# Alternating the convolution's matmul groups with the transposes on TensorE, more of the scaling on ScalarE, and seven load slots in a two-layer convolution kernel

## What is computed

```
def _quantize_per_tensor(t):
    s = jnp.max(jnp.abs(t))
    q = jnp.clip(jnp.round(t * (MAXV / s)), -MAXV, MAXV)
    return (q, s)
...
    qx, sx = _quantize_per_tensor(x)
    qw, sw = _quantize_per_tensor(weight)
    out = lax.conv_general_dilated(qx, qw, window_strides=(1, 1), padding=((1, 1), (1, 1)), dimension_numbers=('NCHW', 'OIHW', 'NCHW'))
    out = out * (sx * sw / (MAXV * MAXV))
    return out + bias.reshape(1, -1, 1, 1)
...
    xf = jnp.fft.rfft2(x, norm='ortho')
    ix = jnp.concatenate([jnp.arange(kX), nX - kX + jnp.arange(kX)])
    xc = xf[:, :, ix, :kY]
    R = jax.lax.complex(R_real, R_imag)
    y = jnp.einsum('ijab,ejab->eiab', R, xc)
    out_f = jnp.zeros_like(xf).at[:, :, ix, :kY].set(y)
    return jnp.fft.irfft2(out_f, s=(nX, nY), norm='ortho')
...
    x = x + _L0_conv_ref(_gn(x), L0_conv_weight, L0_conv_bias)
    x = x + _L1_conv_ref(_gn(x), L1_conv_R_real, L1_conv_R_imag)
```

## Time and profile before

| | |
|---|---|
| median of three runs | 3774.03 us (3768.83 to 3782.59) |
| profiled execution, its own time | 3779.11 us |
| its span in the trace | 3777.3 us |
| mean granted TensorE clock | 0.909 of full speed |
| TensorE busy (matmuls) | 3106.2 us, 82% |
| VectorE busy | 3256.8 us, 86% |
| ScalarE busy | 2350.9 us, 62% |
| GpSimd busy (issuing stores) | 823.0 us, 22% |
| mean DMA rate | 358 GB/s |

### The profile page before, as it was taken

The page is one execution under the profiler, slowest core; times in us unless marked ns, Lnnn a source line. Parts: engine busy times, 40 slices in busy tenths (PEclk is TensorE's granted clock), DMA queues, the critical chain, the costliest instruction groups (busy, mean ns, idle before and its releaser), DMA issues.

```text
span 3777.3 us, 81588 instructions
## 1 busy us (share of the span) xinstructions
PE 3106.2 (82%) x33145; PEld 1541.2 (41%) x33145; DVE 3256.8 (86%) x3336; ACT 2350.9 (62%) x3443; POOL 823.0 (22%) x1040
## 2 busy tenths in 40 slices
PE   5565566569999999999999999878888888888886
PEld 1111111136666666666666666543222222222222
DVE  5878878799999998999999998669888888888887
ACT  5777777768888787878888888643333333333332
POOL 0000000035455454545455454300000000000000
PEclk7767666689999999999999999989999999999998
DMA  9999999999999999999999999749999999999998
GB/s 359 366 359 356 357 361 365 357 250 356 336 319 347 306 354 295 352 306 345 324 332 334 317 346 301 279 170 427 427 427 427 427 427 427 427 423 422 421 421 370
DMA packets 342540, 1352.55 MB, mean 358 GB/s; under 512 B 45792, under 2 KB 47040, under 8 KB 243808
## 3 DMA queue, kind: packets, MB, share of 16 engines
q1 hardware_dynamic: 223104, 811.13, 60.0%
q0 software_dynamic: 82272, 268.58, 19.8%
q10 hardware_dynamic: 36864, 268.45, 16.9%
HBM read 811.10 MB, written 536.87 MB: 357 GB/s over the span
## 4 chain that ended last, share of the span: by engine, by line
DMA 39%; DVE 34%; PE 14%; issue 6%; ACT 5%; SPq 1%; POOL 0%; DVEq 0%; ACTq 0%
DMA out<-ring 19%; DVE ring L561 12%; DMA ring<-in_x 11%; DMA ring<-x_scratch 9%; DVE area L543 6%; ACT area L312 4%; PE ps L721 4%; DVE area L538 4%; PE ps L683 4%; DVE area L547 3%; DVE ring L658 3%; PE ps L732 2%; DVE area L556 2%; PE ps L742 1%; DVE mixb L566 1%
## 5 line engine op out<-in xcount | busy, mean ns | idle before, releaser
L288 POOL DMA_DIRECT2D x_scratch<-ring x1024 | 817.0, 804 | 1596.9 <-DVE ring L561 1574.1
L868 PE MATMUL ps<-x,gj_s 128*128 128x512 bf16 x3072 | 773.6, 406 | 217.2 <-DVE ring L658 216.2
L721 PE MATMUL ps<-area,wq 128*32 128x512 bf16 x12264 | 764.8, 383 | 51.0 <-DVE ring L561 33.7
L658 DVE TENSOR_TENSOR ring<-ps,ring 128x1024 f32<-128x1024 f32 x512 | 603.0, 1219 | 162.5 <-DMA ring<-x_scratch 159.2
L561 DVE SCALAR_TENSOR_TENSOR ring<-ps,sc,ring 128x1024 f32<-128x1024 f32 x512 | 634.2, 1278 | 19.7 <-PE ps L721 12.6
L683 PE MATMUL ps<-ring,negm_s 128*32 128x512 f32 x2048 | 391.4, 905 | 313.4 <-DMA ring<-in_x 313.4
L337 ACT ACTIVATE area<-ps 128x512 f32<-128x512 f32 x1024 | 553.2, 595 | 116.2 <-PE ps L732 115.2
L868 PEld LDWEIGHTS ps<-x,gj_s 128*128 128x128 bf16 x3072 | 294.8, 103 | 773.9 <-DVE ring L658 442.8
L732 PE MATMUL ps<-id_s,ring 128*128 128x128 f32 x4096 | 561.3, 280 | 16.2 <-ACT area L337 14.1
L466 DVE TENSOR_REDUCE stat<-area 128x1 f32<-128x4096 f32 x128 | 559.1, 4410 | 7.1 <-ACT area L312 7.0
L344 ACT ACTIVATE area<-ring,qtab 128x2048 bf16<-128x2048 f32 x256 | 513.1, 2004 | 0.0
(11 more groups left out here) (123 smaller groups left out, 2006.3 us busy)
## 6 DMA issues: line engine op xcount, KB each, us to landing
ring<-in_x SPq DMA_DIRECT2D x256, 1024.0 KB, 7.9
ring<-in_x SPq DMA_DIRECT2D x1024, 256.0 KB, 6.9
x_scratch<-ring POOLq DMA_DIRECT2D x1024, 256.0 KB, 6.6
ring<-x_scratch SPq DMA_DIRECT2D x256, 1024.0 KB, 11.7
out<-ring ACTq DMA_DIRECT2D x256, 1024.0 KB, 25.3
ring<-in_rt SPq DMA_DIRECT2D x1, 4096.0 KB, 15.2
area<-in_gj SPq DMA_DIRECT2D x1, 768.0 KB, 4.7
eh_s<-in_eh SPq DMA_DIRECT2D x1, 128.0 KB, 2.0
```

The source lines that it names most:

```text
L288: pool.dma_start(x1_rows[b, m, r], xslot(t % SL)[32 * r:32 * r + 32, :].rearrange("p (g w) -> p g w", g=4)).then_inc(s_x_out[t % SL], 16)
L658: nc.vector.tensor_tensor(half, ps[0][:, hj * 2 * HW:(hj + 1) * 2 * HW], half, ALU.add).then_inc(s_add, 1)
L721: last = mm(ps[0][32 * cg:32 * cg + 32, HW * g:HW * g + HW], wq[:, (3 * a + dw) * C:(3 * a + dw + 1) * C], src[:, 1 + dw:1 + dw + HW], sta ...
L868: last = mm(bank(j), gj_s[:, (j * 3 + v) * 128:(j * 3 + v + 1) * 128], (z12, z12, z13)[v][:, k % 2], start=(v == 0), stop=(v == 2))
```

## The change

Four things change.

- **Order on TensorE.** `conv` and `turn_x1` are cut into single groups (`conv_group`) and single transposes (`turn_x1` with an argument g). `conv_and_turn` makes, for one half of a chunk, six times: one group of the convolution, then one, one or two transposes of the chunk two behind. The convolution comes first in a step; the width transform stays at its end.
- **Scaling.** ScalarE scales three of a partition's four rows, VectorE one (`UF` in place of `HF`).
- **The small work.** `rows_copied` moves from VectorE to ScalarE; the later small steps come at later values of j, and the loop has five more steps at its end, in which there are no chunks left.
- **Stage 1** has seven load slots in place of four; the new three lie in buffers that stage 1 didn't use. The first chunks of stage 2 wait for the squares of the group that last used their slot.

```
-        def gslot(k):
-            return ring[:, k * FT:(k + 1) * FT]
+            return ring[:, k * FT:(k + 1) * FT] if k < 4 else (vbuf, mixb, x2)[k - 4][:, 0:FT]
...
-                if n >= 4:
-                    sp.wait_ge(s_sq, n - 3)
+                if n >= NGS:
+                    sp.wait_ge(s_sq, n - NGS + 1)
...
-                    sp.wait_ge(s_sq, NT - 3 + t // 2)
+                    sp.wait_ge(s_sq, max(n for n in range(NT) if n % NGS == t // 2) + 1)
...
-                act.activation(u[:, t % 2, 0:HF], xslot(t % SL)[:, 0:HF], ACT.Identity,
+                act.activation(u[:, t % 2, 0:UF], xslot(t % SL)[:, 0:UF], ACT.Identity,
...
+            def rows_copied(b, n):
+                act.wait_ge(s_vt, 8 * b + n + 1)
+                act.activation(vt[:, :, 4 * n:4 * n + 4, :],
+                               bank(7).rearrange("p (c g k) -> p g c k", c=4, g=8), ACT.Copy).then_inc(s_vte, 1)
...
-                nc.vector.tensor_scalar(u[:, t % 2, HF:2 * HF], xslot(t % SL)[:, HF:2 * HF], qtab[:, b:b + 1],
+                nc.vector.tensor_scalar(u[:, t % 2, UF:FC], xslot(t % SL)[:, UF:FC], qtab[:, b:b + 1],
...
+            def conv_group(t, g, dw):
+                if dw == 0 and g == 0:
                     pe.wait_ge(s_q, t + 2)
+                if t and dw == 0 and g % 2 == 0:
+                    pe.wait_ge(s_ev, 2 * (t - 1) + g // 2 + 1)
+                n = 4 * (t % 4) + g
+                above = qs[:, n - 1] if n else (qs[:, 15] if t % TB else qedge)
+                for cg, a, src in ((1, 0, q[:, n]), (2, 1, q[:, n]), (3, 0, qs[:, n]), (0, 1, above)):
+                    last = mm(ps[0][32 * cg:32 * cg + 32, HW * g:HW * g + HW],
+                              wq[:, (3 * a + dw) * C:(3 * a + dw + 1) * C], src[:, 1 + dw:1 + dw + HW],
+                              start=(dw == 0), stop=(dw == 2))
+                if dw == 2 and g % 2:
+                    last.then_inc(s_conv, 1)
+
+            def turn_x1(t, v, g):
+                if g == 0:
+                    if v == 0:
+                        pe.wait_ge(s_ev, 2 * t + 2)
+                    if 4 * t + v >= 2:
+                        pe.wait_ge(s_te, 4 * t + v - 1)
+                last = nc.tensor.transpose(bank(4 + v % 2)[:, 128 * g:128 * g + 128],
+                                           xslot(t % SL)[:, g * HW + 128 * v:g * HW + 128 * v + 128], id_s[:])
+                if g == 3:
+                    last.then_inc(s_t, 1)
+
+            def conv_and_turn(tc, tt, h):
+                turns = [(2 * h + v, g) for v in range(2) for g in range(4)]
+                for k in range(6):
+                    if 0 <= tc < T:
+                        conv_group(tc, 2 * h + k // 3, k % 3)
+                    if 0 <= tt < T:
+                        for v, g in turns[(0, 1, 2, 4, 5, 6)[k]:(1, 2, 4, 5, 6, 8)[k]]:
+                            turn_x1(tt, v, g)
...
-            for i in range(T + 15):
+            for i in range(T + 20):
                 b, j = divmod(i - (TB + 5), TB)
                 small = i >= TB + 5
-                if 4 <= i and i - 4 < T:
-                    turn_x1(i - 4, 0)
-                    turn_x1(i - 4, 1)
-                if 2 <= i and i - 2 < T:
-                    conv(i - 2, 0)
+                conv_and_turn(i - 2, i - 4, 0)
                 if small and j < 4:
                     turn_rows(b, 2 * j)
-                if 4 <= i and i - 4 < T:
-                    turn_x1(i - 4, 2)
-                    turn_x1(i - 4, 3)
-                if 2 <= i and i - 2 < T:
-                    conv(i - 2, 1)
+                conv_and_turn(i - 2, i - 4, 1)
```

More of the change, by code:

```diff
@@ L36, in build @@
     HF = 2 * HW
+    UF = 3 * HW
     FC = NJ * HW
@@ L151, in build @@
         s_rl = sem("r_landed")
-        s_g_in = [sem(f"group_landed{k}") for k in range(4)]
+        s_g_in = [sem(f"group_landed{k}") for k in range(NGS)]
         s_cols = sem("group_column_sums_done")
@@ L372, in _ @@
                     w_copied(i - 6)
-                if small and j == 5:
+                if small and j == 6:
                     h_copied(b)
+                if small and 1 <= j < 5:
+                    rows_copied(b, 2 * j - 1)
                 if 4 <= i and i - 4 < T:
@@ L378, in _ @@
                     squared(i - 4)
+                if small and j < 4:
+                    rows_copied(b, 2 * j)
+                if 4 <= i and i - 4 < T:
                     turned(i - 4, 2)
                     turned(i - 4, 3)
-                if small and j == 8:
+                if small and j == 12:
                     root(b)
@@ L562, in combine @@
                                                op0=ALU.mult, op1=ALU.add).then_inc(s_ev, 1)
[L564 to L567, removed]
             def sums(b):
@@ L598, in _ @@
                     combine(i - 3, 1)
-                if small and 1 <= j < 5:
-                    rows_copied(b, 2 * j - 1)
                 if i < T:
@@ L604, in _ @@
                     nc.vector.memset(qs[64:128, 15, :], 0.0).then_inc(s_q, 1)
-                if small and j < 4:
-                    rows_copied(b, 2 * j)
-                if small and j == 6:
+                if small and j == 8:
                     sums(b)
-                if small and j == 7:
+                if small and j == 11:
                     variance(b)
-                if small and j == 9:
+                if small and j == 14:
                     spectrum(b)
@@ L682, in column_sums @@
                     g = j % 4
-                    last = mm(bank(n % 4)[32 * g:32 * g + 32, :], negm_s[:], gslot(n % 4)[:, j * HW:(j + 1) * HW],
+                    last = mm(bank(n % 4)[32 * g:32 * g + 32, :], negm_s[:], gslot(n % NGS)[:, j * HW:(j + 1) * HW],
                               start=(j < 4), stop=(j >= 4))
@@ L708, in _ @@
             mm(bank(3)[:, 0:2 * B], gsel_s[:], rhs_t[:], start=True, stop=True).then_inc(s_f1p, 1)
-            def conv(t, h):
-                if h == 0:
+            def conv_group(t, g, dw):
+                if dw == 0 and g == 0:
                     pe.wait_ge(s_q, t + 2)
[L714 to L734, removed]
+                if t and dw == 0 and g % 2 == 0:
+                    pe.wait_ge(s_ev, 2 * (t - 1) + g // 2 + 1)
@@ L807, in _ @@
                     along_h1(b)
-                if small and j == 6:
+                if small and j == 7:
                     dc_first(b)
-                if small and j == 7:
+                if small and j == 9:
                     spread(b)
-                if small and j == 9:
+                if small and j == 12:
                     spectra(b)
```

10 lines of the change are left out of this document (6 added, 4 removed).

## The result

The changed kernel takes 4287.3 us (median of four runs, 4284.77 to 4290.33), against 3778.3 us for the kernel before in the same comparison. The ratio is 1.135, with a 95% interval from 1.1315 to 1.138: 13.5% slower. The profiled execution took 4284.77 us, its span is 4283.0.

The account below looks back on a forecast made before the run. VectorE and TensorE were both taken as full in stage 2, with TensorE to bound the new order. Stage 2's +598 us and stage 1's -45 gave a span of 4330, about 4325 us as a median; range 4130 to 4520.

Parts of the forecast that it names:

- The price of changing over: TensorE, stage 2: each change of weight shape, convolution to transposes and back, loses 0.27 us; 8.40 us a chunk, against 5.93.
- the change of order is free: Rival, TensorE in stage 2: transposes load under groups; TensorE needs 4.0 us a chunk, time 3590 or 3730; chance 0.10.
- short blocks cost less: Rival, TensorE in stage 2: pauses partly hidden, a change costs 0.05 us, 7.0 a chunk, time 3970; chance 0.07.
- The clock: Rival, TensorE in stage 2: pauses lower the granted clock; at half throughout, 10.9 us a chunk, time 4960; chance 0.07.
- The small work: TensorE, stage 2: per-image small steps no longer hide behind VectorE and add 12 us an image, 84 us for seven.
- the later values of j cost nothing: Stage 2: moving small steps later is free; ScalarE has 2.7 us free per step.
- Seven slots: Stage 1: more loads in flight fill the gaps, 382 GB/s, 45 us less; at least 0, at most 90.
- Stage 2's window: First to last `combine`: 2134 us of chunks, 5 and 84 more, 2223 us in all against 1625.
- Without that cover: Scaling, stage 2: if TensorE did not cover it, VectorE's 0.3 us would be worth 76 us over 254 steps.

Follow-up runs that it names:

- narrow kernels: narrow_alt and narrow_blocks: the changed kernel with each transpose made by four matmuls with 128 x 32 weights, in two orders; 4401.2 and 4272.2 us.
- slots7: The kernel before with seven load slots in stage 1 and nothing else changed: 3677.2 us, ratio 0.972 to the kernel before.
- blocks: The changed kernel with TensorE's order of before (long blocks of transposes and groups), other edits kept: 3658.9 us, ratio 0.967 to the kernel before.
- six_blocks: The changed kernel with two convolution groups, then two or three transposes, 6 pairs a chunk instead of 12: 3892.3 us, ratio 1.028 to the kernel before.
- narrow_alt: Changed kernel, still alternating, but each 128 x 128 transpose made by four float32 matmuls with 128 x 32 weights: 4401.2 us, ratio 1.164 to the kernel before.
- narrow_blocks: The same narrow transposes as narrow_alt, but in TensorE's order of before (long blocks): 4272.2 us, ratio 1.131 to the kernel before.

## Why the prediction was right, and where it was off

**The price of changing over** was the step that decided, and it was right. Forecast: 0.33 to the transposes, 0.26 behind one, 0.37 behind two, 8.40 us a chunk. Measured: 0.33, 0.26 to 0.27, 0.36 and 8.41. The earlier trace rows held what was needed: in them a load does not start early across a change of shape, and does otherwise. The rule of the Trainium skill, page TensorEngine Tiling, Key Properties, that changing the tiling mode drains the engine, agrees with the traces here: in the changed kernel no load of a transpose starts less than 0.22 us behind the loads of the group before it, in the narrow kernels there is no such pause, and the runs add the price.

**The rivals.** That the change of order is free (3590) fell with the result. Its sum for TensorE was also wrong: 12 x 0.22 + 4 x 0.11 + 0.88 counts four of the sixteen transposes. With all of them it is 5.3 us, not 4.0, and the price below which the change would have paid is (5.93 - 5.3) / 24 = 0.03 us, not 0.08; ScalarE's 5.7 lies above both, so the 3590 did not hang on it. slots7 and blocks show what the other edits give by themselves, 3660 to 3680: near the 3730 that this rival had with the DMA as the bound, less the 58 us that stage 1 gained beyond the forecast. That short blocks cost less fell with the rows above and with six_blocks. The clock stayed at 0.99, so the pauses of 0.1 to 0.2 us did not bring it down.

**The small work** was forecast at 12 us an image; an image takes 281 us, of which 32 x 8.41 = 269 are chunks, so 12. But "the later values of j cost nothing" was read too narrowly. They cost nothing; under the longer step the old values would have cost 138 us, most of it by the granted clock that falls behind the pauses, and the prediction did not look at what they protect.

**Seven slots** was the mis-sized term: 45 us forecast, 103 measured, beyond the bound of 90. I scaled the rate by the share, which assumes that a packet's time stays. The window at 426 GB/s in the earlier trace rows was close to the 421 that the changed kernel then held for hundreds of us, and I took it, reduced to a share of 1.00, for an end and not for the value. The wait for squares that I cited was no measure either: it is 562.5 us of the stretch from 20 to 670 us before, and still 522.1 with five slots, at the full rate. Stage 2's window came out at 2235 in place of 2223. In the measure of the span this 12, the 58 of stage 1 and 1 of stage 3 give 4283 in place of 4330; the two errors have opposite signs, so the total came out a little nearer than stage 1 alone would have put it, by luck.

**Scaling.** "Without that cover worth 76 us" was wrong in its number, though it played no part in the sum: without the cover it is worth 4 us or less, since other limits, the DMA and TensorE, lie right behind.

## What to carry to other kernels

Before interleaving matmuls of different shapes to fill gaps, look at one change of shape in the trace: if the weight load behind it starts only when the matmuls ahead have drained (here 0.11 us lost one way, 0.10 the other, and 0.06 for a bare first load), multiply by the number of changes per step, and group equal shapes into long blocks. When the order or the length of a step in a pipelined loop changes, look again at small work that in-order engines hand to each other: here one engine asked before the other had done its part, and moving the question some steps later was worth 138 us. Count in what the pauses do to the granted clock, which was more than the pauses themselves. Two busy engines and a DMA share of 1.0 can be three limits side by side: relieving one bought nothing here.

## What the hardware showed that I had not expected

**A fifth slot of 2 MB raised the load rate from 362 to 421 GB/s**, more than the idle share explains, and the sixth and seventh added nothing.

**In the narrow kernels TensorE halts for its instructions.** For a transposed piece they have 8 matmuls and 8 loads in the trace where the changed kernel has 1 of each, and their traces show pauses of 1 to 4 us without a releaser. The waits of narrow_alt from 1200 to 2000 us, and the rows of the instruction queue on its page and on that of the changed kernel:

```profile
PE ps L738 <- issue: 52.4, 39, 3.3
...
PE ps L724 <- issue: 27.9, 17, 3.5
PE ps L758 <- issue: 27.2, 20, 3.0
```

```profile
q8 instruction: 460, 7.54, 0.7%
```

```profile
q8 instruction: 236, 3.87, 0.4%
```

Some 107 us of those 800 are such halts of the matmuls, and the instruction queue moved twice the bytes, in packets of 16 KB. Packet by packet the traces show the cause. In the stage 2 windows of narrow_alt and narrow_blocks, 158 and 113 matmuls start behind an idle time of over 1 us without a releaser. Every one of these 271 starts 1.20 to 1.75 us after a packet of the instruction queue has ended; at times drawn at random nine distances in ten lie between 0.3 and 6.2 us. One also stands before the last of the 32 matmuls of a width transform (the row at 1465.86), where the kernel has no wait. So TensorE was out of instructions. blocks has six such halts, 17 us in all, with the same distance, and the changed kernel none. Both narrow kernels move one packet for about 255 of TensorE's matmuls and loads, as the changed kernel does, and so need one twice as often.

Why a packet comes too late for some halts and not for the others stays open. Slow transfers are at most a part of it: in narrow_alt the packets that ended a halt took 1.14 us (median), the others 1.08.
